# Bases 5 to 7, both biases and W1 issued from ScalarE's DMA queue in a two-layer graph network kernel on one core

## The reference, cut to what matters

```python
def _L0_gnn_ref(x, bases, w_comp, h_bias, norm, src, dst, etype):
    weight = jnp.einsum('rb,bio->rio', w_comp, bases)      # 8 bases of 512x512
    h_rel = jnp.einsum('ni,rio->rno', x, weight)
    msg = h_rel[etype, src] * norm
    out = jax.ops.segment_sum(msg, dst, num_segments=n_nodes)
    return out + h_bias

def _L1_gnn_ref(x, edge_index, W, b):                      # loops added, symmetric norm by degree
    h = x @ W.T + b
    out = jax.ops.segment_sum(norm[:, None] * h[row], col, num_segments=n)
    return jax.nn.relu(out)

h = jnp.maximum(_layernorm(x, axis=-1), 0.0)
x = x + _L0_gnn_ref(h, bases, w_comp, h_bias, edge_weight1, src, dst, edge_type_32)
h = jnp.maximum(_layernorm(x, axis=-1), 0.0)
x = x + _L1_gnn_ref(h, edge_index, W, b)
```

## Time and profile before

| what | value |
|---|---|
| median of three runs | 630.19 us (628.79 to 630.42) |
| profiled execution, span from first to last instruction | 625.8 us |
| TensorE busy | 496.4 us (79%) |
| VectorE busy | 328.6 us (52%) |
| POOL busy | 352.2 us (56%) |
| ScalarE busy | 151.9 us (24%) |
| mean granted TensorE clock | 0.905 |
| DMA | 132.82 MB, mean 212 GB/s |
| q1 (SyncE) | 30.99 MB |
| q10 (ScalarE) | 1.13 MB |

### The profile page before, as it was taken

The page is one execution under the profiler, slowest core; times in us unless marked ns, Lnnn a source line. Parts: engine busy times, 40 slices in busy tenths (PEclk is TensorE's granted clock), DMA queues, the critical chain, the costliest instruction groups (busy, mean ns, idle before and its releaser), DMA issues.

```text
span 625.8 us, 15841 instructions
## 1 busy us (share of the span) xinstructions
PE 496.4 (79%) x5824; PEld 317.0 (51%) x5824; DVE 328.6 (52%) x929; ACT 151.9 (24%) x272; POOL 352.2 (56%) x473
## 2 busy tenths in 40 slices
PE   3031445598999899999999998999897876889996
PEld 1020334356666556666656665566564554545443
DVE  7898038885665446636655556645542221544121
ACT  3392234532222122211322202203210000341021
POOL 3334536786676776766747757677677777200000
PEclk9665657599999999999999999999997977789999
DMA  9896965557786887886858868778788788323042
GB/s 283 306 362 216 391 161 150 166 152 211 217 278 202 255 259 205 256 262 175 272 153 252 258 189 262 222 235 273 210 250 261 216 234 240 118 68 102 2 98 68
DMA packets 53427, 132.82 MB, mean 212 GB/s; under 512 B 12173, under 2 KB 18174, under 8 KB 53350
## 3 DMA queue, kind: packets, MB, share of 16 engines
q0 software_dynamic: 27040, 99.60, 53.1%
q1 hardware_dynamic: 25356, 30.99, 15.9%
q10 hardware_dynamic: 954, 1.13, 0.6%
HBM read 120.58 MB, written 11.10 MB: 210 GB/s over the span
## 4 chain that ended last, share of the span: by engine, by line
PE 52%; DMA 14%; DVE 12%; issue 8%; ACT 5%; POOL 5%; SPq 3%; ACTq 1%; POOLq 0%; DVEq 0%
PE PS L1521 22%; PE PS L1501 16%; DMA gath<-rows_layer,srcs 9%; PE PS L1595 7%; POOL gath L722 5%; PE PS L1541 4%; DMA types<-types_by_slot 2%; SPq L579 2%; DVE room_b L1225 2%; ACT room_b L841 2%; DVE zt L1225 1%; DMA edge_records<-room_c 1%; DVE room_b L1261 1%; DMA w1t<-edge_records,w1t 1%; PE PS L1507 1%
## 5 line engine op out<-in xcount | busy, mean ns | idle before, releaser
L722 POOL DMA_INDIRECT gath<-rows_layer,srcs x335 | 335.7, 1002 | 165.1 <-issue 84.8
L1501 PE MATMUL PS<-sel,gath 128*128 128x48 f16 (+7 forms) x4020 | 299.1, 207 | 52.8 <-DMA gath<-rows_layer,srcs 21.8
L1501 PEld LDWEIGHTS PS<-sel,gath 128*128 128x128 f16 x4020 | 235.4, 103 | 163.9 <-issue 86.6
L1521 PE MATMUL PS<-room_b,zt 128*128 128x512 f16 x480 | 168.6, 392 | 1.5 <-DVE sel L1147 1.0
L1521 PE MATMUL PS<-room_b 128*128 128x512 f16 (+1 forms) x480 | 151.7, 384 | 2.0 <-DMA gath<-rows_layer,srcs 1.8
L1141 DVE TENSOR_TENSOR masks<-iota_n,dloc 128x24 bf16<-128x24 f32 (+12 forms) x92 | 17.9, 194 | 96.6 <-issue 58.8
L1507 PE MATMUL PS<-oh_ad,gath 128*128 128x30 bf16 (+7 forms) x335 | 65.1, 194 | 0.0
L782 ACT CAST val<-val_f 128x64 f16<-128x64 f32 x42 | 11.0, 262 | 201.8 <-DVE val_f L1098 196.8
L1521 PEld LDWEIGHTS PS<-room_b 128*128 128x128 f16 (+1 forms) x480 | 47.8, 105 | 16.8 <-DMA gath<-rows_layer,srcs 2.1
L1521 PEld LDWEIGHTS PS<-room_b,zt 128*128 128x128 f16 x480 | 45.2, 100 | 8.6 <-issue 2.2
L1147 DVE TENSOR_TENSOR sel<-masks,val 128x192 f32<-128x192 bf16 (+12 forms) x92 | 38.6, 420 | 0.0
(11 more groups left out here) (202 smaller groups left out, 409.9 us busy)
## 6 DMA issues: line engine op xcount, KB each, us to landing
room_b<-in_L_gnn_bases_dram SPq DMA_DIRECT2D x8, 1024.0 KB, 9.3
gath<-rows_layer,srcs POOLq DMA_INDIRECT x335
types<-types_by_slot SPq DMA_DIRECT2D x168, 16.0 KB
x_t<-x_base SPq DMA_DIRECT2D x19, 128.0 KB
u_t<-in_x_dram SPq DMA_DIRECT2D x9, 256.0 KB, 6.2
x_base<-u_t SPq DMA_DIRECT2D x9, 256.0 KB
x_layer<-x_t SPq DMA_DIRECT2D x18, 128.0 KB
u_t<-x_layer SPq DMA_DIRECT2D x18, 128.0 KB, 2.7
```

What stands on the lines that cost most here:

```text
L722: pool.indirect_dma_start(out=gath[:, s % UN, :], out_offset=None, in_=tab0_d[:, :], in_offset=bass.IndirectOffsetOnAxis(ap=srcs[:, s:s + ...
L1501: mm(there, gath[:, s % UN, D * t + P * f:D * t + P * (f + 1)], sel_parts[:, here, k, 0:NB * w, u], start=first and t == 0 and u == 1, sto ...
L1521: last = mm(PS[0:r, PBANK[q], :], zt[q % 2][:, t, f, b, 0:r], base_hl[:, b, u, f, :], start=(m == 0), stop=(m == NM - 1))
```

## The change

The loop that loads bases 5 to 7 and the loads of both biases leave SyncE's program and stand in ScalarE's, behind the last cast of the table and before the squares of bases 0 to 4. W1's wait and load leave SyncE's program and stand in ScalarE's behind the set-up, before its list of steps. Transfers, targets and semaphores are the same.

```diff
@@ SyncE
             for v in range(1, TRING):
                 load_types(v)
-            for n in range(BEARLY, NB):
-                load_base(n)
-            sp.dma_start(hb_t[:, :], h_bias.rearrange("(p d) -> p d", p=1).to_broadcast([P, D])).then_inc(s_bias, 16)
-            sp.dma_start(b1_t[:, :], b1.rearrange("(p d) -> p d", p=1).to_broadcast([P, D])).then_inc(s_bias, 16)
...
-            sp.wait_ge(s_tab0, 16 * (NT + 3))
-            sp.dma_start(w_in, W1.rearrange("(c p) i -> p c i", p=P)).then_inc(s_win, 16)
             sp.wait_ge(s_xbase, 16 * NT)
             for v in range(TRING, TRING + VEARLY):
                 load_types(v)
@@ ScalarE
             high(NT - 1)
 
+            for n in range(BEARLY, NB):
+                act.dma_start(base_in[:, n + 2, :, :], bases[n, :, :].rearrange("(f p) o -> p f o", p=P)).then_inc(s_bin[n], 16)
+            act.dma_start(hb_t[:, :], h_bias.rearrange("(p d) -> p d", p=1).to_broadcast([P, D])).then_inc(s_bias, 16)
+            act.dma_start(b1_t[:, :], b1.rearrange("(p d) -> p d", p=1).to_broadcast([P, D])).then_inc(s_bias, 16)
+
             def val_hi(v):
...
                 act.wait_ge(s_any_out, 96 * NT)
+
+            act.wait_ge(s_tab0, 16 * (NT + 3))
+            act.dma_start(w_in, W1.rearrange("(c p) i -> p c i", p=P)).then_inc(s_win, 16)
 
             def flush(r):
```

## The result

The changed kernel takes 621.54 us, the median of four runs (620.31 to 623.13), against 630.31 us of the kernel before beside them: ratio 0.9872, 95% interval 0.9836 to 0.9909, 8.8 us faster. The profiled execution has a span of 618.4 us, 7.4 less than before, and took 620.31 us. In every run for which both were recorded the time is 1.8 or 1.9 us above the span, not 4.4: the profile shown of before was of one of its faster executions (its spans in later runs lie between 624.0 and 630.6).

A forecast was written before the change was run, and what follows sets the result against it. Bound: block 3's types queued behind some 4.7 MB on SyncE, idling TensorE 13.4 us. -13.4 + 2.2 = -11.2 us; span 625.8 - 11.2 = 614.6, plus 4.4 around it: 619.0 us, range 615.5 to 625.6.

The forecast's parts named there:

- part 1: SyncE's queue: without the long loads, block 3's types land in time and TensorE's wait before its lookup goes, -13.4 us.
- late next: Before the transpose: after the types, W1's square is late next, done by 73, against slots 0 to 6 ending at 73.5.
- part 2: ScalarE: five added issues take 3.6 us, hidden in its 4.65 us wait for VectorE; cost taken as nothing.
- part 3: Table's rows: the moved loads share the DMA engines with them, delaying types, first gather and slot 0; cost +2.2 us.
- SyncE's kept 58%: Share of bytes assumed for SyncE's queue beside ScalarE's: 220 GB/s, table's rows 2.1 us late.
- The row of 13 to 17 us: Earlier stretch where both queues had work: ScalarE's moved 0.64 MB, SyncE's 0.89; source of the assumed share.
- The even split of bytes: Table's rows: alternative reading of the skill page, a delay of 4.4 us instead of 2.2 and a forecast of 621.2.
- 8.07 us of TensorE's sequencing: Between block 2's lookup and slot 0: taken as TensorE's own fixed time, moving slot 0 from 64.67 to 66.9.
- part 4: W1 on ScalarE: issued about 61.7, landed at 70 to 71, squared by 73; transpose at 74.7; loss taken as nothing.
- Less: Rival: ScalarE's loads crowd SyncE's queue by up to 6.1 us, issuing is held or gather 7 late; 623 to 625.7; 0.18.
- Only issue time: Rival: types and W1 land by total bytes, so only SyncE's 4.7 us of issue is won; 625.5; chance 0.05.
- Slower: Rival: ScalarE held in issuing, deciding from some 14 us, less cover costing one for one; +6.6, 637; chance 0.04.

The follow-up runs named there:

- order alone: Kernel before, with the types of blocks 3 to 5 issued ahead of bases 5 to 7, biases and W1, all in SyncE's queue; 634.28 us.
- late bytes: Changed kernel, with bases 5 to 7 and the biases issued by ScalarE only after the table is in, right ahead of W1; 634.88 us.
- W1 early: Changed kernel, with W1 issued by ScalarE as soon as the table is in, ahead of value blocks 1 and 2; 618.76 us.
- small packets: Against bases only: each of ScalarE's bases loaded as four DMAs of 128 columns, packets of 512 B instead of 2 KB; 617.83 us.
- bases only: Kernel before, with bases 5 to 7 alone moved to ScalarE's queue; biases and W1 stay with SyncE; 618.72 us.

## Why the prediction was right in the main, and which steps failed

**Removing the types' wait (part 1): right, -13.4 us.** With the long loads elsewhere VectorE no longer waits for block 3, and the lookup follows slot 6 at once. That it counts only together with W1's earlier landing was in the forecast as "late next"; the runs with the order alone (+4.0 us) and with the late bytes (+4.7) show how much hung on it.

**ScalarE's five issues (part 2): mis-sized, and still free.** 7.1 us (0.42 + 1.16 + 2.35 + 3.13) against 3.6. The fifth square ended at 55.4, past the old time of value block 0 (53.39), but VectorE itself was 5.4 us late by then, so nobody waited.

**The table's rows (part 3): the term that failed.** "SyncE's kept 58%" gave 2.1 us; the first gather came 5.8 us later (60.11), near the upper bound of 6.1. SyncE issued the table's last rows hardly later than before (at 50.5 us, against 50.2), as VectorE's low halves set that. The delay lies in their landing; in the chain of work that ended last it is one piece:

```profile
50.48 7.94 DMA rows_layer<-room_c
```

The queues after the change, first from 42 to 44 us, then from 42 to 50:

```profile
q10 hardware_dynamic: 305, 0.62, 86.6%
q1 hardware_dynamic: 303, 0.09, 18.9%
```

```profile
q10 hardware_dynamic: 1010, 2.01, 66.1%
q1 hardware_dynamic: 983, 1.15, 39.6%
```

SyncE's queue moved 36% of the bytes, not 58%, while the counts of packets are within 3% of each other. Right ahead of the table's rows stood the types of all slots on their way to DRAM, in packets of some 300 B, each of which gave way to 2 KB of a base; SyncE waits for just that store before it issues the types of block 0, at 45.60 instead of 42.36. From 44 to 56 us SyncE's queue moved 2.08 of 4.85 MB, and by 57.5 us all 3.67 MB of ScalarE's loads were through, ahead of the table's last rows (58.4). The row of 13 to 17 us was misread: from 13 to 14 us ScalarE's queue had hardly begun (16 packets, against 839 of SyncE's). From 14.5 to 16 us of the kernel before, where both had work, it holds what the changed kernel showed later, nearly equal counts and 37% of the bytes for SyncE:

```profile
q10 hardware_dynamic: 113, 0.38, 62.7%
q1 hardware_dynamic: 127, 0.22, 37.9%
```

The Trainium skill, "DMA: Bandwidth & Descriptors", section "Queues, rings and completion order", has the engines change queues by the packet; the trace agrees wherever both queues had work, with 2 KB against 300 B (305 and 303) as with 512 B on ScalarE's side (894 and 901). The even split of bytes that the prediction put beside its own value, 4.4 us, was nearer than the 2.2; it has no place for packets of 300 B.

**From the table to slot 0.** The forecast added its delay one for one (66.9); it was 68.17, +3.5. The "8.07 us of TensorE's sequencing" was wrong: after the change 6.4 us lie between lookup and slot 0, and TensorE waits for VectorE's selects in them. Part of the old 8 us was another wait. Two runs bear on it: with the order alone and with the late bytes the table and the lookup were as early as before (lookup at 56.54 and 56.39), but no base moved beside the first gathers (bases issued from 61.23 and 59.01), and slot 0 came at 62.95 and 62.43 instead of 64.67, 6.4 and 6.0 us behind the lookup instead of 8.4. So some 2 us of slot 0's time before was the price of the bases beside the first gathers; no row shows the landing of gather 0 itself. That slot 0 missed the forecast by only 1.3 us is luck: the lookup was 5.5 us later instead of 2.2, and these 2 us, which nobody had counted, came back.

**W1 and the gathers (part 4): the second term that failed.** I had W1 issued at 61.7 and landed by 71; it was issued at 64.38 and landed at 76.8. It stood behind value block 2, which had slipped with the types of block 1, and met the gathers. From 68 to 71 us after the change:

```profile
q10 hardware_dynamic: 323, 0.66, 76.6%
q1 hardware_dynamic: 111, 0.17, 20.2%
q0 software_dynamic: 23, 0.06, 6.6%
```

The gathers (q0) all but stopped. The one of slot 4, issued at 65.13, took 9.72 us, and slot 4 waited 2.96 us for it, where the forecast had put a late gather at nothing (bound 2.7, for gather 7). The transpose, at 78.98 for 74.7, met the end of slot 7 and W1's square (78.8) together. The run with W1 early undoes both and takes 2.8 us less. Why the gathers got so little in those 3 us while eight of them were issued by 70.5 stays open.

**The sum.** -13.4, + 3.5 for slot 0, + 3.0 for slot 4's gather: -6.9 at the transpose, where the profile has it; -7.2 at slot 13, -7.4 in the span, -8.8 in the medians. The forecast had -11.2 at the transpose and missed it by 4.3 us; that the medians miss by only 2.5 is the scatter between executions and no merit of the sum. That the shift would reach the end held in all fourteen profiles, to within 2.6 us.

**The rivals.** The measured 621.54 lies in the forecast's own range (617.5 to 622), but the signs say that *Less*, at 623 to 625.7, had the better mechanism: ScalarE's loads crowded SyncE's queue by nearly the 6.1 us, and a gather was late. Of the forecast's signs, the first gather (58 or later was to mean *Less*), the longest wait for types (5.4 us, for 3), slot 0 (68.17, for 68 at most), W1's square (from 76.8, for an end before 74) and slot 13 (89.83, for 88 at most) all fell on that side. On the forecast's side were slot 7 right behind slot 6 and the 4.7 MB on ScalarE's queue, and none of its signs of being wrong appeared. *Only issue time* fell: 8.8 us is more than 4.7, and the time came from bytes moved into the idle stretch of 44 to 50. Yet the rule of the Trainium skill beside it ("DMA: Bandwidth & Descriptors", "Issuing engines are not separate DMA queues") stands: in the run with a queue of its own and late bytes the types no longer waited, but spreading alone won no time. *Slower* was tried unawares: with small packets ScalarE was held 17 us, past the 14 from which it was to decide, and that kernel, which leaves W1 and the biases with SyncE, was 1.9% faster than before. The price of one for one was wrong for it: its squares began 16.7 us later than before, but VectorE waited only 4.9 us for ScalarE's first value block, as the late types had held VectorE back too.

## What to carry to other kernels

When a small load waits behind large ones in an in-order queue, look for the next thing that needs the large ones before counting the whole wait as won: here two waits ended 1.3 us apart, and putting the small loads first, with the large ones 7 us later for it, made the kernel 4 us slower. What paid was moving bytes into a stretch in which the DMA engines idled; the second queue was the means here. A second hardware queue is not subordinate to the first: what is put there is to be counted as going packet for packet with it, and small packets in the first queue lose most. Here that cost the first gather 4.4 to 5.8 us and still paid. Issue what is needed last-but-one (here W1) the moment its space is free. Of the kernels tried, bases only (618.7), W1 early (618.8) and small packets (617.8) have medians 2.8 to 3.7 us below the changed kernel's and can't be told from each other; only those of bases only lie below it in every run, and the intervals of all three ratios touch its own.

## What the runs showed of the hardware that I had not expected

Two hardware queues with 2 KB packets moved the same number of packets to within 3% (1010 and 983, 1016 and 1010 in 8 us), also when one held 300 B packets (305 and 303 in 2 us) or 512 B ones (894 and 901 in 4 us). So a queue's share of the bytes went by the size of its packets. An issue can hold its engine: 3.13 us for a 256 KB load as the fifth large one of ScalarE, 17.06 us for eleven DMAs of 512 B packets. The same 1 MB load took 5.4, 6.6, 12.4 and 15.2 us to land, by what shared the engines with it.
